# Half of each cross-attention head's probability tiles turned by VectorE in 32x32 squares and carried to their partitions by DMA

## The chip, the cores and the metric

The kernel runs on one core of one Trainium2 chip. The metric is the device time in microseconds of the whole program. The profiled execution is a separate one, with its own time.

## The reference

A decoder layer in float32 on x (8 batches, 512 tokens, 512 features) and a context of the same size: self-attention with one wide head, cross-attention with 16 heads of 64, a mixture-of-experts feed-forward, and a layer norm after each. What the change touches is the cross-attention:

```python
q = (Q @ Wq + bq).reshape(b, len_q, H, DIM_K).transpose(0, 2, 1, 3)
k = (K @ Wk + bk).reshape(b, K.shape[1], H, DIM_K).transpose(0, 2, 1, 3)
v = (V @ Wv + bv).reshape(b, V.shape[1], H, DIM_V).transpose(0, 2, 1, 3)
att = jnp.einsum('bhqd,bhkd->bhqk', q * scale, k)
att = jax.nn.softmax(att, axis=-1)
out = jnp.einsum('bhqk,bhkd->bhqd', att, v)
out = out.transpose(0, 2, 1, 3).reshape(b, len_q, H * DIM_V)
return out @ Wo + bo
```

There are 8 x 16 = 128 pairs of batch and head. Each has a 512 x 512 matrix of probabilities.

## The kernel before

Three stages run one after the other: self-attention, cross-attention (`cross_attention`), feed-forward. Float32 products are made of float32r parts: a value is split into a high part and the rest (hi and lo), and a projection takes three products of 512 columns for each of four chunks of the contraction, 12 matmuls in all.

The cross-attention goes through 16 groups (`GROUPS`; one half of the heads times one batch) of 8 heads, and a group has 16 steps, two to a head. The order is written out by hand: `SCHEDULE` gives each step at most one projection item (V, K, Q of the next heads or groups, O of the group before). In a step TensorE does the 12 matmuls of the item (`project`, L1311), the scores of two tiles of a head that is two to three steps ahead (`scores`, L1324, 4 matmuls), the products of probabilities and values of two tiles (`values`, L1348, 4 matmuls), and the turns of two tiles (`turn`, L1335, 8 transposes). A tile of scores is 128 queries x 512 keys. It goes from PSUM through VectorE (`max_tile`, L1122), ScalarE (`exp_tile`, L1019, which also sums the row), VectorE (`recip`, L1128) and GpSimd (`norm_tile`, L958) into `prob`, which holds two heads. A turned tile is 128 keys x 512 queries, made of four 128x128 transposes into one PSUM bank; ScalarE copies its high part into `pt` (`pt_hi_tile`, L1047) and VectorE the rest (`pt_lo_tile`, L1168). After a head's four `values` ScalarE (`o_first`, L1054) and VectorE (`o_second`, L1178) bring the output to `osum`, and GpSimd splits it (`split_out`, L972 and L974).

Each engine executes its own list in order and waits for semaphores. SyncE (SP) issues all DMAs: each weight pair after the projection before it (`load_pair`, L844), the copies of the keys from one half of the partitions to the other (`double_k`, L859, from SBUF to SBUF), context (L164), x1T (L841), values' weights (L172), and the loads and stores of y (L847, L851).

## Time and profile before

| | us |
|---|---|
| median of 3 runs | 1960.04 (1959.64 to 1960.54) |
| the profiled execution | 1960.26 |
| its span, first to last instruction | 1958.4 |
| TensorE busy | 1941.7 (99%) |
| VectorE busy | 1475.2 (75%) |
| ScalarE busy | 1149.4 (59%) |
| GpSimd busy | 729.5 (37%) |

Busy times of one row can overlap in a pipelined engine, so the time from one instruction's start to the next one's start says more than the mean duration. In the digit rows each digit is a fortieth of the span. Of 16 DMA engines the share is the time that packets took.

### The profile page before, as it was taken

The numbers are of one execution on the slowest core, as the hardware profiler recorded it, in microseconds if no ns is written. First come the engines' busy times: TensorE is split into PE (matmuls) and PEld (weight loads), VectorE is DVE, ScalarE is ACT, GpSimd is POOL, SyncE is SP. The second block draws the span as 40 slices with busy tenths as digits, with TensorE's granted clock in tenths as the row PEclk, the third lists the DMA queues.
The fourth block names the chain that finished last, engine by engine and source line by source line (L and its number), as shares of the span: only waits on it lengthen the run. The fifth ranks groups of instructions, "written<-read, shape, count | busy, mean of one in ns | idle before, by whom it ended". The sixth has DMA issues, their size and how long they took to land.

```text
span 1958.4 us, 29643 instructions
## 1 busy us (share of the span) xinstructions
PE 1941.7 (99%) x9856; PEld 1632.4 (83%) x9856; DVE 1475.2 (75%) x3134; ACT 1149.4 (59%) x2462; POOL 729.5 (37%) x858
## 2 busy tenths in 40 slices
PE   8999999999999999999999999999999999999998
PEld 7888888788888888888888888888888888788887
DVE  5676666787777777777777777777777788867887
ACT  5445544676666666666766666666666667632221
POOL 2322342132343433332333333333333343527763
PEclk9999999999999999999999999999999999999999
DMA  5777778863556536364553726355462636321221
GB/s 215 274 285 280 300 280 318 277 218 106 185 171 189 186 116 195 98 192 140 184 168 101 237 65 215 107 162 172 119 193 66 194 115 218 130 87 44 86 87 65
DMA packets 112086, 334.87 MB, mean 171 GB/s; under 512 B 9152, under 2 KB 9152, under 8 KB 107200
## 3 DMA queue, kind: packets, MB, share of 16 engines
q1 hardware_dynamic: 111936, 332.98, 51.2%
q8 instruction: 80, 1.31, 0.3%
q14 instruction: 70, 0.57, 0.1%
HBM read 211.31 MB, written 88.08 MB: 153 GB/s over the span
## 4 chain that ended last, share of the span: by engine, by line
PE 94%; DVE 2%; ACT 2%; issue 1%; DMA 0%; POOL 0%; ACTq 0%; DVEq 0%; POOLq 0%
PE a_proj L1311 17%; PE a_turned L1311 17%; PE a_score L1324 11%; PE a_av L1348 11%; PE a_proj L48 9%; PE a_proj L1335 5%; PE a_turned L1335 5%; PE a_proj L1739 4%; PE a_av L1739 4%; PE a_score L48 3%; PE a_av L48 3%; ACT c_prob L1019 1%; PE a_score L1714 1%; PE a_turned L1698 1%; PE a_turned L612 1%
## 5 line engine op out<-in xcount | busy, mean ns | idle before, releaser
L958 POOL TENSOR_SCALAR c_prob<-c_prob,all_rden 128x512 f32<-128x512 f32 x512 | 350.2, 698 | 881.8 <-DVE all_rden L1128 881.8
L1019 ACT ACTIVATE c_prob<-a_score,all_negmax 128x512 f32<-128x512 f32 x512 | 348.0, 685 | 211.6 <-DVE all_negmax L1122 208.8
L1122 DVE TENSOR_REDUCE all_negmax<-a_score 128x1 f32<-128x512 f32 x512 | 329.3, 685 | 186.4 <-PE a_score L1324 186.1
L1324 PE MATMUL a_score<-c_ks,c_qs 128*128 128x512 f32 x1024 | 277.6, 391 | 3.3 <-ACT c_prob L1019 3.0
L1348 PE MATMUL a_av<-c_pt,c_vs 128*128 128x512 f32 x1024 | 277.1, 391 | 0.0
L1324 PEld LDWEIGHTS a_score<-c_ks,c_qs 128*128 128x128 f32 x1024 | 190.5, 188 | 44.7 <-ACT c_prob L1019 5.9
L1348 PEld LDWEIGHTS a_av<-c_pt,c_vs 128*128 128x128 f32 x1024 | 192.0, 188 | 39.8
L1168 DVE TENSOR_TENSOR c_pt<-a_proj,c_pt 128x512 fp32r<-128x512 f32 x258 | 171.9, 686 | 27.0 <-ACT c_pt L1047 25.0
L1311 PE MATMUL a_proj<-all_second_buffer,c_wq 128*128 128x512 f32 x756 | 188.0, 397 | 0.0
L1311 PE MATMUL a_turned<-all_third_buffer,all_first_buffer 128*128 128x512 f32 x732 | 182.6, 398 | 0.0
L1168 DVE TENSOR_TENSOR c_pt<-a_turned,c_pt 128x512 fp32r<-128x512 f32 x254 | 169.1, 686 | 9.0 <-ACT c_pt L1047 5.3
L1311 PEld LDWEIGHTS a_proj<-all_second_buffer,c_wq 128*128 128x128 f32 x756 | 137.4, 188 | 26.0
L1311 PEld LDWEIGHTS a_turned<-all_third_buffer,all_first_buffer 128*128 128x128 f32 x732 | 133.0, 188 | 25.6
L1047 ACT CAST c_pt<-a_proj 128x512 fp32r<-128x512 f32 x258 | 144.8, 589 | 1.9 <-PE a_proj L1335 1.9
L1335 PE MATMUL a_proj<-all_ident,c_prob 128*128 128x128 f32 x1032 | 144.9, 272 | 0.2 <-POOL c_prob L958 0.2
L1047 ACT CAST c_pt<-a_turned 128x512 fp32r<-128x512 f32 x254 | 143.1, 593 | 1.4
L1335 PE MATMUL a_turned<-all_ident,c_prob 128*128 128x128 f32 x1016 | 142.6, 272 | 0.1
L1311 PE MATMUL a_proj<-all_first_buffer,c_wk 128*128 128x512 f32 x564 | 141.2, 399 | 0.0
L1335 PEld LDWEIGHTS a_proj<-all_ident,c_prob 128*128 128x128 f32 x1032 | 122.8, 140 | 18.1 <-POOL c_prob L958 0.5
L1335 PEld LDWEIGHTS a_turned<-all_ident,c_prob 128*128 128x128 f32 x1016 | 120.9, 140 | 18.0 <-POOL c_prob L958 0.6
L1311 PE MATMUL a_turned<-c_WO,c_op 128*128 128x512 f32 x540 | 134.9, 398 | 0.0
L1039 ACT ACTIVATE c_qs<-a_proj,all_bq 64x512 fp32r<-64x512 f32 x126 | 86.4, 686 | 71.7 <-PE a_proj L1311 70.1
(207 smaller groups left out, 3275.0 us busy)
## 6 DMA issues: line engine op xcount, KB each, us to landing
all_first_buffer<-ctxT_scratch SPq DMA_DIRECT2D x64, 512.0 KB, 7.4
c_wk<-wk_scratch SPq DMA_DIRECT2D x64, 512.0 KB, 3.8
c_wq<-wq_scratch SPq DMA_DIRECT2D x64, 512.0 KB, 6.1
all_second_buffer<-x1T_scratch SPq DMA_DIRECT2D x16, 2048.0 KB, 14.8
c_ks<-c_ks SPq DMA_DIRECT2D x128, 256.0 KB, 5.6
ctxT_scratch<-s_csp SPq DMA_DIRECT2D x8, 2048.0 KB, 7.4
c_y<-y_steps_scratch SPq DMA_DIRECT2D x16, 1024.0 KB, 6.1
y_steps_scratch<-c_y SPq DMA_DIRECT2D x15, 1024.0 KB, 10.0
```

The costliest lines, as they stand in the source:

```text
L48: ins = nc.tensor.matmul(out, stationary(s, k), moving(m, k), start=(k == 0 and s == m == HI), stop=((k, (s, m)) == last))
L958: nc.gpsimd.tensor_scalar(prob[:, n % 2, i, :], prob[:, n % 2, i, :], rden[:, n % 2, i:i + 1], 1.0, ALU.mult, ALU.mult).then_inc(p_ready, 1)
L1019: nc.scalar.activation(prob[:, n % 2, i, :], spsum[:, i % 2, :], ACT.Exp, bias=negmax[:, n % 2, i:i + 1], scale=1.0, accum_out=den[:, n % ...
L1039: nc.scalar.activation(dst, bank[rows, :], ACT.Identity, bias=bias[rows, bass.ds(G * PAIRS + j, 1)], scale=1.0).then_inc(proj_hi, 1)
L1047: nc.scalar.copy(pt[:, t % LAG, HI, :], bank_of(("T", g, t))).then_inc(pt_hi, 1)
L1122: nc.vector.tensor_reduce(negmax[:, n % 2, i:i + 1], spsum[:, i % 2, :], AX.X, ALU.max, negate=True).then_inc(smax, 1)
L1168: nc.vector.tensor_tensor(pt[:, t % LAG, LO, :], bank_of(("T", g, t)), as_f32(pt[:, t % LAG, HI, :]), ALU.subtract).then_inc(pt_lo, 1)
L1311: ins = nc.tensor.matmul(bank_of(item), l, r, start=(k == 0 and s == m == HI), stop=(k == K - 1 and (s, m) == TERMS[-1]))
L1324: ins = nc.tensor.matmul(spsum[:, i % 2, :], qs[:, j % 2, e, i * P:(i + 1) * P], ks[:, j % 2, e, m, :], start=(m == HI), stop=(m == LO))
L1335: ins = nc.tensor.transpose(bank_of(("T", g, t))[:, i * P:(i + 1) * P], prob[:, n % 2, i, k * P:(k + 1) * P], ident[:, :])
L1348: ins = nc.tensor.matmul(opsum[:, n % 2, :], vs[:, g % 2, k, n, :], pt[:, t % LAG, m, :], start=(k == 0 and m == HI), stop=(k == T - 1 and ...
L1739: ins = pe.matmul(prod[i % 2][:, which, :], x2T[u][:, s, k, i * P:(i + 1) * P], W[which][:, m, k, :], start=(k == 0 and s == m == HI), sto ...
```

## The change

The last two of a head's four tiles of keys (`FLIPPED`, 2) are no longer turned by TensorE. For 125 of the 128 heads (all but `WHOLE`, the first two and the last):

- `prob` is laid out as [P, S, T] in place of [P, T, S]: the four query tiles stand side by side, so each of them is read and written with a step of 16 bytes. This holds for the exponentials, the scaling on GpSimd, TensorE's remaining transposes, whose output in the PSUM bank has a step of 16 bytes too (`squares`), and the sum of `o_second`, which puts the order right.
- VectorE turns the keys 256 to 511 of each query tile in place in squares of 32x32 (`flip`): four transposes of 128x256 a head.
- SyncE sends the squares to their partitions (`send_flips`): sixteen DMAs a head, each 32 partitions x 2 x 128 numbers (32 KB, runs of 512 bytes) from `prob` to `landing`, half of them in each of two steps.
- ScalarE copies the landed tiles' high part (`flip_hi_tile`, two 128x512 copies from SBUF) and GpSimd subtracts (`flip_lo_tile`, two 128x512).
- `exp_tile` of a head waits until the sixteen DMAs of the head two before have landed, since they read the same half of `prob`.
- The order of TensorE changes: `turned_in` has one turned tile a step in place of two, and `valued_in` three tiles of values in the even steps and one in the odd ones, the flipped ones four steps after the head's turn has begun. `MIDDLE` is another order of the items, with Q1 in the next group.
- The loads of context, x1T, WV and WO are issued by ScalarE in pieces (`BULK`: steps 3, 4, 6 to 11) instead of by SyncE. x1T goes in four pieces.
- In the feed-forward's preparation the stores go in pieces, `pool_gate` comes later, and several semaphores `passed` are one.

```diff
-    TILES, STEPS, LEAD, LAG = T * HH, T * HH // 2, 4, 4
+    TILES, STEPS, LEAD = T * HH, T * HH // 2, 4
+    Q, TURNED, FLIPPED = 32, 2, 2
+    SQUARES = P // Q
...
-    NEXT = ["V0+", "K0+", "Q0+", "V1+", "V2+", "K1+", "Q1+"]
-    MIDDLE = ["V3", "K2", "Q2", "O0", "O1", "O2", "K3", "Q3", "O3"] + NEXT
+    NEXT = ["V0+", "K0+", "Q0+", "V1+", "K1+", "V2+"]
+    MIDDLE = ["Q1", "K2", "Q2", "V3", "O0", "O1", "K3", "Q3", "O2", "O3"] + NEXT
...
+    WHOLE = (0, 1, HH * GROUPS - 1)
+    def turned_in(g, step):
+        n, half = divmod(step, 2)
+        return [(g, T * n + k) for k in ((2 * half, 2 * half + 1) if HH * g + n in WHOLE else (half,))]
+    def valued_in(g, step):
+        n, half = divmod(step, 2)
+        tiles = [(n - 1, 1)] if half else [(n - 2, 2), (n - 2, 3), (n - 1, 0)]
+        return [x for x in (tile_of(g, *tile) for tile in tiles) if x]
...
+    def send_flips(g, n, places=range(SQUARES)):
+        head = HH * g + n
+        sp.wait_ge(flipped, T * FLIPS[head])
+        wait(sp, av_mm, T * (head - 1))
+        src = prob[:, n % 2, TURNED * P:, :].rearrange("p (k c q) i -> p c k (q i)", k=FLIPPED, c=SQUARES)
+        dst = as_f32(landing[:, head % 2, :, :]).rearrange("p k (a n) -> p a k n", a=SQUARES)
+        for a in places:
+            for c in range(SQUARES):
+                sp.dma_start(dst[c * Q:(c + 1) * Q, a], src[a * Q:(a + 1) * Q, c]).then_inc(landed[head % 2], 16)
...
+        if head:
+            send_flips(*head, range(2, SQUARES) if step % 2 else range(2))
+        if item and item[0] == "K":
+            double_k(item[1], item[2])
...
+    def flip_lo_tile(g, n, k):
+        nc.gpsimd.tensor_tensor(whole, as_f32(whole), as_f32(flip_hi_part[:, k, :]), ALU.subtract).then_inc(flip_lo, 1)
...
+    BULK = {3: [("v", (0, 1))], 4: [("v", (2, 3))], 10: [("o", (0, 1))], 11: [("o", (2, 3))], 6: [("c", 0), ("c", 1)], 7: [("c", 2), ("c", 3)], 8: [("x", 0), ("x", 1)], 9: [("x", 2), ("x", 3)]}
...
         if i == 0:
-            wait(act, t_mm, T * head - T)
-        nc.scalar.activation(prob[:, n % 2, i, :], spsum[:, i % 2, :], ACT.Exp,
+            if head - 2 in FLIPS:
+                act.wait_ge(landed[head % 2], 16 * SQUARES * SQUARES * LANDINGS[head - 2])
+        nc.scalar.activation(prob[:, n % 2, :, i], spsum[:, i % 2, :], ACT.Exp,
...
+    def flip_hi_tile(g, n, k):
+        act.wait_ge(landed[head % 2], 16 * SQUARES * SQUARES * LANDINGS[head])
+        wait(act, av_mm, T * (head - 1) + TURNED + k + 1)
+        nc.scalar.copy(flip_hi_part[:, k, :], as_f32(landing[:, head % 2, k, :])).then_inc(flip_hi, 1)
...
+    def flip(g, t):
+        dve.wait_ge(p_ready, TILES * g + t + 1)
+        block = prob[:, n % 2, TURNED * P:, i]
+        nc.vector.transpose(block, block).then_inc(flipped, 1)
...
-            ins = nc.tensor.transpose(bank_of(("T", g, t))[:, i * P:(i + 1) * P],
-                                      prob[:, n % 2, i, k * P:(k + 1) * P], ident[:, :])
+            ins = nc.tensor.transpose(squares(bank_of(("T", g, t)))[:, i], prob[:, n % 2, k * P:(k + 1) * P, i],
+                                      ident[:, :])
```

TensorE in the middle of the cross-attention, before: a step with the item Q and the beginning of the next one. Names are the written and the read tiles; `a_proj`, `a_score`, `a_turned`, `a_av` are PSUM banks.

```order
L1311 MATMUL a_proj<-all_second_buffer,c_wq 128x512 x12
L1324 MATMUL a_score<-c_ks,c_qs 128x512 x4
L1348 MATMUL a_av<-c_pt,c_vs 128x512 x4
L1335 MATMUL a_turned<-all_ident,c_prob 128x128 x8
L1311 MATMUL a_proj<-c_WO,c_op 128x512 x12
```

And after: an odd step, and then an even one.

```order
L1367 MATMUL a_proj<-c_WO,c_op 128x512 x12
L1380 MATMUL a_score<-c_ks,c_qs 128x512 x4
L1406 MATMUL a_av<-c_pt,c_vs 128x512 x2
L1390 MATMUL a_proj<-all_ident,c_prob 128x128 x4
L1367 MATMUL a_turned<-all_third_buffer,all_first_buffer 128x512 x12
L1380 MATMUL a_score<-c_ks,c_qs 128x512 x4
L1406 MATMUL a_av<-c_flip_hi,c_vs 128x512
L1406 MATMUL a_av<-c_landing,c_vs 128x512
L1406 MATMUL a_av<-c_flip_hi,c_vs 128x512
L1406 MATMUL a_av<-c_landing,c_vs 128x512
L1406 MATMUL a_av<-c_pt,c_vs 128x512 x2
L1390 MATMUL a_turned<-all_ident,c_prob 128x128 x4
```

The eight transposes of a step are now four; the 20 matmuls of 512 columns are 18 in the odd step and 22 in the even one.

SyncE (SP) before, over most of a group: the DMAs in order, with the semaphores that the first of a row waits for.

```order
L844 DMA c_wk<-wk_scratch 128x1024 [waits c_proj_mm]
L164 DMA all_first_buffer<-ctxT_scratch 128x2x512 x4
L859 DMA c_ks<-c_ks 64x1024 [waits c_proj_lo] x2
L844 DMA c_wq<-wq_scratch 128x1024 [waits c_proj_mm]
L841 DMA all_second_buffer<-x1T_scratch 128x4096
L851 DMA y_steps_scratch<-c_y 128x4x512 [waits c_wo_out]
L847 DMA c_y<-y_steps_scratch 128x4x512 [waits c_y_stored]
```

And after, in some six steps of a group, from the second half of one head's sixteen on:

```order
L903 DMA c_landing<-c_prob 32x2x128 [waits c_av_mm,c_flipped,c_proj_mm]
L903 DMA c_landing<-c_prob 32x2x128 x7
L880 DMA c_y<-y_steps_scratch 128x4x512 [waits c_y_stored]
L877 DMA c_wk<-wk_scratch 128x1024 [waits c_proj_mm]
L903 DMA c_landing<-c_prob 32x2x128 [waits c_av_mm,c_flipped]
L903 DMA c_landing<-c_prob 32x2x128 x7
L891 DMA c_ks<-c_ks 64x1024 [waits c_proj_lo] x2
L903 DMA c_landing<-c_prob 32x2x128 [waits c_av_mm,c_flipped,c_proj_mm]
```

Context and x1T are gone from this queue, and eight DMAs stand in each step, with the weights' loads ahead of them and the copies of the keys behind them.

ScalarE after, one even step and the odd step behind it:

```order
L1084 ACTIVATE c_qs<-a_turned,all_bq 64x512 [waits c_s_mm,c_proj_mm]
L1084 ACTIVATE c_qs<-a_turned,all_bq 64x512
L1064 ACTIVATE c_prob,all_den<-a_score,all_negmax 128x512 [waits c_landed1,c_t_mm,c_smax]
L1064 ACTIVATE c_prob,all_den<-a_score,all_negmax 128x512 [waits c_smax]
L1112 ACTIVATE c_opart<-a_av,all_bv 64x512 [waits c_o_sum,c_av_mm]
L1099 CAST c_pt<-a_turned 128x512 [waits c_av_mm,c_t_mm]
L1105 CAST c_flip_hi<-c_landing 128x512 [waits c_av_mm,c_landed1] x2
L1076 CAST c_vs<-a_proj 128x8x64 [waits c_proj_mm]
L1064 ACTIVATE c_prob,all_den<-a_score,all_negmax 128x512 [waits c_smax] x2
L1099 CAST c_pt<-a_proj 128x512 [waits c_av_mm,c_t_mm]
```

The exponential that waits for `landed` has everything else of ScalarE behind it.

## Rows read from the trace of the kernel before

**Rows 1.** The page: busy times, the granted clock, the DMA queue.

```profile
PE 1941.7 (99%) x9856; PEld 1632.4 (83%) x9856; DVE 1475.2 (75%) x3134; ACT 1149.4 (59%) x2462; POOL 729.5 (37%) x858
...
PEclk9999999999999999999999999999999999999999
...
q1 hardware_dynamic: 111936, 332.98, 51.2%
```

**Rows 2.** The page's chain that ended last, shares of the span by engine.

```profile
PE 94%; DVE 2%; ACT 2%; issue 1%; DMA 0%; POOL 0%; ACTq 0%; DVEq 0%; POOLq 0%
```

**Rows 3.** Line 1335 alone: duration ns min/median/max, first and last start.

```profile
L1335 PE MATMUL a_proj<-all_ident,c_prob x1032: 270/272/332, 367.5 to 1732.0; 128*128 128x128 f32 x172
...
L1335 PE MATMUL a_turned<-all_ident,c_prob x1016: 270/272/328, 366.8 to 1724.4; 128*128 128x128 f32 x170
```

**Rows 4.** Timeline, 1000 to 1015 us: start, us, engine, line, count.

```profile
1000.56 1.07 PE L1348 MATMUL a_av<-c_pt,c_vs 128*128 128x512 f32 x4
1001.25 1.02 PEld L1335 LDWEIGHTS a_turned<-all_ident,c_prob 128*128 128x128 f32 x8
...
1001.48 1.03 PE L1335 MATMUL a_turned<-all_ident,c_prob 128*128 128x128 f32 x8
...
1002.24 2.58 PEld L1311 LDWEIGHTS a_proj<-all_second_buffer,c_wq 128*128 128x128 f32 x12
1002.27 2.98 PE L1311 MATMUL a_proj<-all_second_buffer,c_wq 128*128 128x512 f32 x12
...
1005.08 1.07 PE L1324 MATMUL a_score<-c_ks,c_qs 128*128 128x512 f32 x4
```

**Rows 5.** The page's costliest groups: count, busy, mean ns.

```profile
L1019 ACT ACTIVATE c_prob<-a_score,all_negmax 128x512 f32<-128x512 f32 x512 | 348.0, 685 | 211.6 <-DVE all_negmax L1122 208.8
...
L1168 DVE TENSOR_TENSOR c_pt<-a_proj,c_pt 128x512 fp32r<-128x512 f32 x258 | 171.9, 686 | 27.0 <-ACT c_pt L1047 25.0
...
L1047 ACT CAST c_pt<-a_proj 128x512 fp32r<-128x512 f32 x258 | 144.8, 589 | 1.9 <-PE a_proj L1335 1.9
L1335 PE MATMUL a_proj<-all_ident,c_prob 128*128 128x128 f32 x1032 | 144.9, 272 | 0.2 <-POOL c_prob L958 0.2
```

**Rows 6.** Busy us of each engine in a stretch of the cross-attention.

```profile
560.00:1000.00 440.00, 440.00 (x2266) 370.43 (x2265) 336.52 (x648) 289.42 (x628) 160.83 (x219) 1.00 0.51 161
```

**Rows 7.** Groups by line and shape: the nearest to the added operations.

```profile
L974 POOL TENSOR_TENSOR c_op<-c_osum,c_op 128x512 fp32r<-128x512 f32 x60 | 77.5, 1292 | 5.0
...
L368 ACT CAST s_wsp<-s_wraw 128x512 fp32r<-128x512 f32 x32 | 17.5, 617 | 0.3
```

**Rows 8.** VectorE's groups by shape, 256 and 512 columns.

```profile
L488 DVE TENSOR_TENSOR all_x<-a_score,s_strip 128x512 f32<-128x512 f32 x8 | 5.5, 689 | 7.8 <-PE a_score L48 7.8
...
L488 DVE TENSOR_TENSOR all_x<-a_score,s_strip 128x256 f32<-128x256 f32 x8 | 3.4, 424 | 0.3
...
L517 DVE TENSOR_SCALAR s_gone<-all_x 128x256 f32<-128x256 f32 x8 | 2.2, 274 | 0.0
```

**Rows 9.** Timeline of SyncE's queue, 738 to 746 us.

```profile
738.57 0.33 SPq L844 DMA_DIRECT2D c_wk<-wk_scratch  x1
738.94 1.99 SPq L164 DMA_DIRECT2D all_first_buffer<-ctxT_scratch  x4
741.00 1.38 SPq L859 DMA_DIRECT2D c_ks<-c_ks  x2
```

**Rows 10.** The same, 966 to 973 us.

```profile
967.19 2.53 SPq L172 DMA_DIRECT2D all_third_buffer<-wv_scratch  x4
```

**Rows 11.** Line 859 alone: issue ns, and us to landing.

```profile
L859 SPq DMA_DIRECT2D c_ks<-c_ks x128: 462/468/1127, 348.6 to 1696.3; - x128
...
DMA to landing us min/median/max: 3.0/5.6/12.3
```

**Rows 12.** The page's DMA issues: count, KB each, us to landing.

```profile
y_steps_scratch<-c_y SPq DMA_DIRECT2D x4, 256.0 KB, 2.0
```

**Rows 13.** Waits from 600 to 1700 us: total, times, longest.

```profile
POOL c_prob L958 <- DVE all_rden L1128: 699.2, 205, 5.3
ACT c_prob L1019 <- DVE all_negmax L1122: 162.4, 115, 3.0
```

405 lines of the change are left out of this document (200 added, 205 removed).

## The prediction

> **What bounds the kernel now.** I read the page first. TensorE is busy for 1941.7 us of 1958.4, at full granted clock in every slice, and VectorE for 75% [rows 1]. The chain of work that ended last is TensorE for 94% [rows 2]. The busy share of a pipelined engine can flatter, so I looked at starts: in the timeline the four products with values begin at 1000.56, the eight turns at 1001.48, the next projection at 1002.27, the next scores at 1005.08, with no hole [rows 4]. In the stretch from 560 to 1000 us TensorE is busy throughout [rows 6], and in the list of waits it stands in no long row: GpSimd and ScalarE wait [rows 13]. So here time goes by TensorE's work, as long as the others stay inside it. The turns run from 366.8 to 1732.0 us in 256 steps [rows 3]; less the 0.8 us of the last step's own eight, that is 1364.4 / 255 = 5.35 us a step, 10.70 a head. A matmul of 512 columns costs (1001.48 - 1000.56) / 4 = 0.23 us between starts.
>
> **What the change removes.** 125 heads x 2 tiles x 4 = 1000 transposes. A transpose's price between weight loads is (1002.24 - 1001.25) / 8 = 0.124 us [rows 4]; between matmul starts 0.79 / 8 = 0.099; by busy time 144.9 / 1032 = 0.140 [rows 5]. I take 0.124: -124 us, ends -99 and -140. The step becomes 5.35 - 0.50 = 4.85, the head 9.70 us. Values move by two matmuls from odd steps to even ones, so even steps are about 5.3 and odd ones 4.4.
>
> **What it adds, per step, against 4.85 us.**
> VectorE: 336.52 / 440 x 5.35 = 4.09 now [rows 6]. One `pt_lo` goes, 171.9 / 258 = 0.67 [rows 5]. Two transposes of 128x256 come. No row shows one; the nearest 256-column passes take 0.274 and 0.424 us [rows 8], and twice the second, 0.85, is my upper end, 0.27 the lower. I take 0.35: 4.12. At 0.85 it would be 5.1, above TensorE.
> ScalarE: 289.42 / 440 x 5.35 = 3.52 [rows 6]; one copy from PSUM goes (144.8 / 258 = 0.56, [rows 5]), one from SBUF comes (0.62, [rows 7]), and eight DMAs a group at 0.515 (below), 0.26 a step: 3.84. Step 7 of a group is the worst: two landed tiles 1.24, a Q item some 1.4, two exponentials 2 x 348.0 / 512 = 1.36 [rows 5], a copy 0.56 and two DMA issues 1.03 make 5.6 in a step of 4.4. That lateness of 1.2 in 15 groups is 18 us if TensorE feels all of it; the steps around have room, so I take 8 (ends 0 and 18).
> GpSimd: 160.83 / 440 x 5.35 = 1.96, plus one subtraction of 1.29 [rows 7]: 3.25. It waited 699 us [rows 13]; hidden.
>
> **SyncE.** Sixteen DMAs a head are new. Four loads of context take from 738.94 to 741.00, 0.515 us each [rows 9]; four of values' weights take 2.53, 0.63 each [rows 10]; the only DMA from SBUF to SBUF there is, the copy of the keys, is 0.468 [rows 11] plus a gap of 0.04 (738.57 + 0.33 to 738.94, [rows 9]). The flips are SBUF to SBUF with a stepped second dimension. I take 0.515, by the two rows that agree; ends 0.47 and 0.65. That is 8.24 us a head. What else SyncE issues for a group is eight weight pairs at 0.37, eight copies at 0.51 and two DMAs of y like the pairs: 7.8, so 0.98 a head. Sum 9.2 of 9.70: it fits, narrowly. It stops fitting at (9.70 - 0.98) / 16 = 0.545 us an issue.
>
> **The added waits.** The sends of head n begin when the values of head n-2 are done, 20 matmuls into the head's first step, 4.6 us. Behind that wait stand the weight pairs and key copies. The sends with one weight load (0.37) and half of a pair of key copies (0.5) take 9.1: 13.7. For the landing, DMAs of 256 KB took 2.0 us at best [rows 12], the key copies 3.0 [rows 11]; for 32 KB after its issue I take 1.5 (ends 1.0 and 3.0): 15.2. The first exponential of head n+2, which must wait for that, would start by itself after two steps, 14 matmuls and a maximum: 9.7 + 3.2 + 0.7 = 13.6. So it starts 1.6 late. Behind it on ScalarE stands everything, but TensorE needs the result only at its scores a step later, at 9.7 + 5.3 + 2.8 = 17.8, so the start may be as late as 17.1. Margin 1.9 us. Also around the loop (release, the exponentials and copies of two steps, GpSimd's scaling, the flip: some 8 us with hand-offs; then 9.1 and 1.5): 18.6 for two heads, 9.3 each, under 9.70. Heads in whose steps a weight load and both key copies come, or that meet ScalarE's bulk transfers on the DMA engines, use the margin up. For these I take 0.28 us a head, 35 us (ends 0 and 110, the latter by 0.9 a head).
>
> **DMA engines.** 125 heads x 512 KB is 65.5 MB; by bytes 65.5 / 333 x 51.2% = 10% more [rows 1], hidden. By packets (125 x 16 x 64 = 128,000 of 512 bytes, beside 111,936) it would be 58% more, over the whole: that is the far end. I stay near bytes.
> The Trainium skill ("DMA: Bandwidth & Descriptors", Why small descriptors are slow) says that SBUF-to-SBUF transfers do not suffer the penalty of small descriptors; no row here shows runs of 512 bytes between partitions.
>
> **Sum.** The profiled execution, 1960.3 (0.2 over the median): - 124 + 8 + 35 = 1879 us.
>
> **Stepped access.** The exponential's output, the scaling, the flips, the weight loads of the remaining transposes and their output in PSUM now step by 16 bytes. No row shows such an access. I price it at nothing, as all rows are of contiguous ones; the other end is that each such element takes twice the time.
> The Trainium skill ("SBUF — State Buffer", Door 1: The DMA port swizzle) says that accesses want at least two hits in a 16-byte line of SBUF and that any non-contiguous pattern in PSUM slows matmuls significantly. With fp32 and a step of 16 bytes every access would be to another line. No row here can weigh it; it speaks against the change, for the rival next.
>
> **Rivals.**
> 1. Stepped access costs. If the eight transposes that a head keeps take 0.248 instead of 0.124, TensorE's head is again 9.70 + 0.99 = 10.69, what it was. An element costs VectorE (689 - 424) / 256 = 1.04 ns [rows 8]; with as much on ScalarE an exponential takes 0.5 us more: 3.84 + 1.0 = 4.9 a step; VectorE some 0.27 more a flip and 0.27 a step for the sum: 4.9. Nobody has slack, and the loop grows by four exponentials' 2.0 and 0.6 elsewhere, to 10.6 a head. Time 1960 to 1990; I say 1975. If only half of it holds, about 1925. For it: nothing measured. Against it: nothing measured.
> 2. SyncE becomes the bound. At the row with 0.645 us from start to start (2.53 us and its gap, for four, [rows 10]) a head costs 16 x 0.645 + 0.98 = 11.3 us against 10.70 before: 125 x 0.6 = 75 us slower, 2035. It decides against the change from (10.70 - 0.98) / 16 = 0.607 us an issue. For it: that row has the same stepped form, and landing times of up to 12.3 us show queues [rows 11]. Against it: the other two rows.
> 3. VectorE becomes the bound: transposes of 0.85 make its step 5.12, 0.27 over TensorE's: 250 x 0.27 = 68 us above the forecast, 1947. For it: VectorE has the largest share beside TensorE. Against it: a pass of 256 columns takes half of that.
>
> **Chances.** Forecast 0.41 (own range 1845 to 1925); stepped access 0.26, of which 0.06 still faster, 0.04 within, 0.16 slower; SyncE or the DMA engines 0.21, slower; VectorE 0.12, of which 0.05 faster, 0.01 within, 0.06 slower (the sum of stepped access on top). A measurement of this kernel tells 0.2%, 4 us, from no change. Faster 0.52, within 0.05, slower 0.43. The range takes in the -140 with nothing lost below and the SyncE case above: 1840 to 2040.
>
> **What would show it.** Right: TensorE's step at 4.85, four transposes in 0.5 us between the weight loads' starts; L903 at 0.5 us from start to start; the exponential's wait for `landed` short, with TensorE not waiting for it; VectorE's transposes at 0.3 to 0.4. Wrong: weight loads of L1390 well above 140 ns or exponentials above 685 ns (rival 1); SyncE issuing without a pause and TensorE idle behind ScalarE's exponential (rival 2); VectorE busy for over 95% of a step (rival 3). If TensorE idles for long, the granted clock in its row may leave 9; a chain with much less TensorE than 94% would say so as well.

## The result and the profile after

The changed kernel takes 2300.16 us (2297.74 to 2303.30, four runs) against 1960.12 for the kernel before in the same comparison: a ratio of 1.1735, 95% interval 1.1721 to 1.1749. The forecast was 1879 us with a range up to 2040. It failed by 421 us and in its sign.

| us | before | after |
|---|---|---|
| span of the profiled execution | 1958.4 | 2300.2 |
| TensorE busy | 1941.7 (99%) | 2022.9 (88%) |
| VectorE busy | 1475.2 (75%) | 1651.6 (72%) |
| ScalarE busy | 1149.4 (59%) | 1329.6 (58%) |
| GpSimd busy | 729.5 (37%) | 1298.9 (56%) |

The page of the changed kernel, the rows that answer to [rows 1]:

```profile
PE 2022.9 (88%) x8856; PEld 1579.2 (69%) x8856; DVE 1651.6 (72%) x3384; ACT 1329.6 (58%) x2462; POOL 1298.9 (56%) x1108
...
PEclk9999999899999999999999999999999899889999
...
DMA packets 288932, 400.58 MB, mean 174 GB/s; under 512 B 42112, under 2 KB 170112, under 8 KB 286592
...
q1 hardware_dynamic: 252864, 329.44, 45.3%
```

TensorE is busy for longer although a tenth of its instructions is gone, and no engine is busy for over 88%: everything waits for something. The chain that ended last, which was TensorE for 94% [rows 2]:

```profile
PE 34%; SPq 34%; DVE 10%; DMA 8%; issue 6%; ACT 6%; POOL 2%; ACTq 1%; POOLq 0%; DVEq 0%
SPq L903 30%; DMA c_landing<-c_prob 8%; PE a_proj L48 8%; PE a_turned L1367 4%; ACT c_prob L1064 4%; PE a_proj L1789 4%; PE a_av L1789 4%; DVE all_negmax L1183 3%; PE a_score L48 3%; PE a_av L48 2%; DVE c_prob L1237 2%; PE a_score L1380 2%; SPq L877 2%; DVE c_osum L1246 2%; PE a_proj L1367 2%
```

A third of it is now SPq, the issue of transfers on SyncE's queue, and nearly all of that is line 903, the sends. The costliest groups, which answer to [rows 5, 7]:

```profile
L985 POOL TENSOR_SCALAR c_prob<-c_prob,all_rden 128x512 f32<-128x512 f32 x512 | 608.6, 1214 | 644.6 <-DVE all_rden L1189 644.3
L1064 ACT ACTIVATE c_prob<-a_score,all_negmax 128x512 f32<-128x512 f32 x512 | 564.5, 1176 | 580.0 <-DMA c_landing<-c_prob 500.7
L1380 PE MATMUL a_score<-c_ks,c_qs 128*128 128x512 f32 x1024 | 351.9, 446 | 210.4 <-ACT c_prob L1064 208.4
...
L992 POOL TENSOR_TENSOR c_landing<-c_landing,c_flip_hi 128x512 fp32r<-128x512 f32 x250 | 318.7, 1298 | 12.7 <-ACT c_flip_hi L1105 11.9
...
L1237 DVE STREAM_TRANSPOSE c_prob<-c_prob 128x256 f32<-128x256 f32 x500 | 303.1, 651 | 26.4 <-POOL c_prob L985 26.1
L1246 DVE TENSOR_TENSOR c_osum<-a_av,c_opart 64x512 f32<-64x512 f32 x128 | 141.9, 1109 | 61.6 <-ACT c_opart L1112 61.4
...
L1105 ACT CAST c_flip_hi<-c_landing 128x512 fp32r<-128x512 f32 x250 | 143.1, 625 | 0.0
...
L1390 PEld LDWEIGHTS a_turned<-all_ident,c_prob 128*128 128x128 f32 x532 | 93.8, 202 | 67.1 <-POOL c_prob L985 54.4
```

Two things stand here. ScalarE's exponential waited 500.7 us for landings, and the scores 208.4 us for the exponential. And every operation that steps by 16 bytes is longer: the exponential 1176 ns against 685, the scaling 1214, the sum of `o_second` 1109, the flip 651, the weight loads of the turns 202. The operations that do not step are as priced: the copy of a landed tile 625, GpSimd's subtraction 1298.

The busy times of the stretch from 700 to 1700 us, in the columns of [rows 6]:

```profile
700.00:1700.00 1000.00, 865.18 (x3646) 651.11 (x3644) 734.50 (x1367) 646.49 (x1175) 628.75 (x539) 0.96 0.58 168
```

Less TensorE (865 of 1000 against 440 of 440), and a granted clock of 0.96 where it was 1.00, in a stretch in which the engine pauses for the exponential. A matmul of the scores takes 446 ns here in the mean, 391 before. What part of the lost time is the lower clock, and not the pauses before it, no run separates. Line 903 alone (issue ns min/median/max, who waited, landing):

```profile
L903 SPq DMA_DIRECT2D c_landing<-c_prob x2000: 585/597/2087, 395.0 to 2059.3; - x182
...
  ACT c_prob L1064: 500.7, 107
...
DMA to landing us min/median/max: 1.8/2.3/9.6
```

The issues themselves stand in the timeline of SyncE and ScalarE around 1200 us (start, us, engine, line, count), as [rows 9, 10] for before:

```profile
1198.98 8.96 SPq L903 DMA_DIRECT2D c_landing<-c_prob  x14
...
1207.99 0.59 SPq L880 DMA_DIRECT2D c_y<-y_steps_scratch  x1
...
1208.62 0.50 SPq L877 DMA_DIRECT2D c_wk<-wk_scratch  x1
1209.22 5.08 SPq L903 DMA_DIRECT2D c_landing<-c_prob  x8
1209.30 1.17 ACT L1064 ACTIVATE c_prob<-a_score,all_negmax 128x512 f32<-128x512 f32 x1 [3.37 <-DMA c_landing<-c_prob]
...
1210.87 2.39 POOL L985 TENSOR_SCALAR c_prob<-c_prob,all_rden 128x512 f32<-128x512 f32 x2 [3.37 <-DVE all_rden L1189]
```

Fourteen sends take 8.96 us, eight take 5.08: 0.64 us from start to start, and the neighbours, a load of y and of a weight pair, are as close. From 700 to 1700 us the trace holds 1402 transfers of SyncE, 1221 of them sends, and the pauses between them sum up to 66 us. So 16 x 1000 / 1221 = 13.1 us a head against 10.70 before, and (13.1 - 10.7) x 125 = 300 of the 340 us that were lost. The exponential at 1209.30 has waited 3.37 us for the landing of the head two before, whose last send was issued at 1207.35 and landed 1.8 us later: it waits for SyncE to get through its list. VectorE's reciprocal and GpSimd's scaling wait behind it. The list of waits from 700 to 1500 us, which answers to [rows 13] (total, times, longest), has that at the top:

```profile
ACT c_prob L1064 <- DMA c_landing<-c_prob: 241.5, 55, 12.4
DVE all_rden L1189 <- ACT c_prob L1064: 149.9, 69, 9.5
PEld a_score L1380 <- ACT c_prob L1064: 131.2, 117, 8.7
```

### The profile page after: what moved, and what is told of

Its sections match the earlier page's. It is cut to its first block, busy times and chain, and to the rows that moved or that the text cites. A ratio compares the mean times of both kernels' runs of the same rounds, so it can differ in the third digit from the quotient of the medians.

```text
span 2300.2 us, 30421 instructions
## 1 busy us (share of the span) xinstructions
PE 2022.9 (88%) x8856; PEld 1579.2 (69%) x8856; DVE 1651.6 (72%) x3384; ACT 1329.6 (58%) x2462; POOL 1298.9 (56%) x1108
## 2 busy tenths in 40 slices
DMA packets 288932, 400.58 MB, mean 174 GB/s; under 512 B 42112, under 2 KB 170112, under 8 KB 286592
## 4 chain that ended last, share of the span: by engine, by line
PE 34%; SPq 34%; DVE 10%; DMA 8%; issue 6%; ACT 6%; POOL 2%; ACTq 1%; POOLq 0%; DVEq 0%
SPq L903 30%; DMA c_landing<-c_prob 8%; PE a_proj L48 8%; PE a_turned L1367 4%; ACT c_prob L1064 4%; PE a_proj L1789 4%; PE a_av L1789 4%; DVE all_negmax L1183 3%; PE a_score L48 3%; PE a_av L48 2%; DVE c_prob L1237 2%; PE a_score L1380 2%; SPq L877 2%; DVE c_osum L1246 2%; PE a_proj L1367 2%
## 5 line engine op out<-in xcount | busy, mean ns | idle before, releaser
L985 POOL TENSOR_SCALAR c_prob<-c_prob,all_rden 128x512 f32<-128x512 f32 x512 | 608.6, 1214 | 644.6 <-DVE all_rden L1189 644.3
L1064 ACT ACTIVATE c_prob<-a_score,all_negmax 128x512 f32<-128x512 f32 x512 | 564.5, 1176 | 580.0 <-DMA c_landing<-c_prob 500.7
L1380 PE MATMUL a_score<-c_ks,c_qs 128*128 128x512 f32 x1024 | 351.9, 446 | 210.4 <-ACT c_prob L1064 208.4
L992 POOL TENSOR_TENSOR c_landing<-c_landing,c_flip_hi 128x512 fp32r<-128x512 f32 x250 | 318.7, 1298 | 12.7 <-ACT c_flip_hi L1105 11.9
L1237 DVE STREAM_TRANSPOSE c_prob<-c_prob 128x256 f32<-128x256 f32 x500 | 303.1, 651 | 26.4 <-POOL c_prob L985 26.1
L1246 DVE TENSOR_TENSOR c_osum<-a_av,c_opart 64x512 f32<-64x512 f32 x128 | 141.9, 1109 | 61.6 <-ACT c_opart L1112 61.4
L1367 PE MATMUL a_turned<-all_second_buffer,c_wq 128*128 128x512 f32 x564 | 146.5, 410 | 0.0
L1105 ACT CAST c_flip_hi<-c_landing 128x512 fp32r<-128x512 f32 x250 | 143.1, 625 | 0.0
L1367 PE MATMUL a_proj<-all_third_buffer,all_first_buffer 128*128 128x512 f32 x564 | 141.1, 399 | 0.6 <-DVE c_ks L1208 0.6
L1367 PEld LDWEIGHTS a_turned<-all_second_buffer,c_wq 128*128 128x128 f32 x564 | 107.5, 198 | 21.1
L1064 ACT ACTIVATION_READ_ACCUMULATOR c_prob<-a_score,all_negmax 128x1 f32 x512 | 111.1, 217 | 0.0
```

The source lines that it names most:

```text
L985: nc.gpsimd.tensor_scalar(prob[:, n % 2, :, i], prob[:, n % 2, :, i], rden[:, n % 2, i:i + 1], 1.0, ALU.mult, ALU.mult).then_inc(p_ready, 1)
L992: nc.gpsimd.tensor_tensor(whole, as_f32(whole), as_f32(flip_hi_part[:, k, :]), ALU.subtract).then_inc(flip_lo, 1)
L1064: nc.scalar.activation(prob[:, n % 2, :, i], spsum[:, i % 2, :], ACT.Exp, bias=negmax[:, n % 2, i:i + 1], scale=1.0, accum_out=den[:, n % ...
L1237: nc.vector.transpose(block, block).then_inc(flipped, 1)
L1246: nc.vector.tensor_tensor(osum[rows, n // 2, :].rearrange("p (i a q) -> p i a q", i=T, a=SQUARES), squares(opsum[DK:P, n % 2, :]), squares ...
L1367: ins = nc.tensor.matmul(bank_of(item), l, r, start=(k == 0 and s == m == HI), stop=(k == K - 1 and (s, m) == TERMS[-1]))
```

## The experiments

Every kernel ran beside the kernel before on the same chip (1960.0 to 1960.8 us). The theories at the start: SyncE's queue is full; the sends land late or are slow for another reason; the 16-byte step. "Does not cross" below means that the squares stay in their partitions. The stretches and lists of waits are from 700 to 1500 us.

### 1. Fewer transfers, the step alone, the order alone

`one_send`: the sixteen sends of a head become one of the same bytes, which does not cross, issued in the head's second step. `four_sends`: four of them, one for each 32 partitions.

```diff
-        for a in places:
-            for c in range(SQUARES):
-                sp.dma_start(dst[c * Q:(c + 1) * Q, a], src[a * Q:(a + 1) * Q, c]).then_inc(landed[head % 2], 16)
+        if 0 in places:
+            return
+        sp.dma_start(as_f32(landing[:, head % 2, :, :]),
+                     prob[:, n % 2, TURNED * P:, :].rearrange("p (k m) i -> p k (m i)", k=FLIPPED)).then_inc(
+                         landed[head % 2], 16)
```

> Left out: the squares are not carried across partitions; one DMA a head of 128 partitions carries the same 512 KB in place of the sixteen. All else is the changed kernel. SyncE theory (SyncE's list of DMAs, at 0.64 to 0.68 us each, sets the pace of 13.1 us a head): SyncE's work falls from some 12.4 to under 3 us a head, TensorE's own work becomes the bound at some 10.0 us a head, time 1850 to 1930, ScalarE waits for landed under 30 us in all. Stepped-access theory (the slower exponentials, scalings and sums set the pace): time stays over 2150. Latency theory (the round from a head's landing to the next but one's flips is too long, whatever SyncE does): between the two, 2000 to 2150, and ScalarE still waits for landed.

> Left out: crossing partitions; four DMAs a head of 32 partitions x 2 x 512 numbers, each to its own partitions, two in each step, the same bytes. SyncE theory: 4 x 0.65 + 1.6 = 4.2 us a head on SyncE, no bound, within 1% of the kernel with one send. Latency theory: a quarter of the way from it to 2300, some 2000. Stepped access: over 2150. It also shows what a 32-partition DMA of four times the bytes takes to issue: 0.6 if it goes by the DMA, 1.2 or more if it goes by bytes or runs.

Measured: 2022.4 us, ratio 1.0323 (1.0307 to 1.0340), and 2061.5, ratio 1.0518 (1.0502 to 1.0533). One transfer in place of sixteen is worth 278 us, but neither comes below the kernel before, where the SyncE theory had put one_send. Both lie near the latency theory's times (2000 to 2150, and some 2000). In one_send SyncE pauses for some 850 of 1000 us, and ScalarE still waits for landings:

```profile
ACT c_prob L1064 <- DMA c_landing<-c_prob: 70.1, 17, 6.6
```

`before_stepped` is the kernel before with only the layout of the change (in SBUF, in the bank in PSUM, and in the sum).

```diff
-    prob = sc.sb("prob", [P, 2, T, S])
+    prob = sc.sb("prob", [P, 2, S, T])
-        nc.scalar.activation(prob[:, n % 2, i, :], spsum[:, i % 2, :],
+        nc.scalar.activation(prob[:, n % 2, :, i], spsum[:, i % 2, :],
...
```

> The kernel before with only the changed kernel's layout: probabilities with the query tile innermost (steps of 16 bytes), transposes into PSUM with the same step, the sum that puts the order right. Nothing left out, no flips. SyncE theory: exponentials 1.0 us apart in place of 0.68, but TensorE stays the bound and grows by what the stepped transposes take, 8 x 0 to 0.04 us a step: 1960 to 2045. Stepped-access theory: most of the 340 us is here, 2200 or more.

Measured: 2004.8 us, ratio 1.0229 (1.0214 to 1.0244), within the SyncE theory's range. The step alone costs 44 us where TensorE is the bound. Its page has TensorE's busy time and these groups:

```profile
PE 1971.8 (98%) x9856; PEld 1669.7 (83%) x9856; DVE 1537.6 (77%) x3134; ACT 1339.2 (67%) x2462; POOL 981.7 (49%) x858
```

```profile
L1019 ACT ACTIVATE c_prob<-a_score,all_negmax 128x512 f32<-128x512 f32 x512 | 571.8, 1189 | 210.4 <-DVE all_negmax L1122 208.9
...
L1337 PEld LDWEIGHTS a_proj<-all_ident,c_prob 128*128 128x128 f32 x1032 | 151.6, 208 | 13.8 <-POOL c_prob L958 4.1
```

The turns from 700 to 1500 us (TensorE's busy time and count, its weight loads' busy time and count, clock, DMA share and GB/s), first before, then here:

```profile
700.00:1500.00 800.00, 152.28 (x1176) 137.10 (x1176) 1.00 0.49 152
```

```profile
700.00:1500.00 800.00, 160.90 (x1152) 161.52 (x1152) 1.00 0.48 150
```

At eight a step that is 147 steps and 144, 5.44 us a step and 5.56, and TensorE is busy for 800.00 of 800 us in both. So some 20 to 30 of the 44 us are TensorE's own turns, eight of which take 0.87 us in place of 0.79 to the start of the next projection. The rest falls in the first and the last groups, which have fewer items for TensorE; from 1690 us to the end of the turns it is busy for 76 of 86 us.

`all_whole` was meant as the order alone: the change with `WHOLE = tuple(range(HH * GROUPS))`, no flips and no sends.

> The changed kernel with every head whole: no flip and no send, all transposes on TensorE, but its order of TensorE, its layout and ScalarE's issuing of the bulk loads. Nothing left out. SyncE theory: like the kernel before with the stepped layout, within 1.5%. A theory that the new order or ScalarE's bulk loads cost: over 2100.

Measured: 2201.3 us, ratio 1.1235 (1.1216 to 1.1254). The number is the second theory's (over 2100), but the list of waits shows another stall, which whole heads alone have in this order, since two of their tiles use buffers that the order releases late:

```profile
ACT c_flip_hi L1099 <- PE a_av L1406: 111.9, 64, 8.0
```

So it says nothing on the flipped heads, and it is no control. `straight_early` below, which has the new order and ScalarE's loads too, is faster than the kernel before, so these two are not what costs.

### 2. The step in the changed kernel, twelve sends, and the way through DRAM

`straight_one` is one_send with the layout of the kernel before. `twelve_sends` keeps the bytes and does not cross.

```diff
         for a in places:
-            for c in range(SQUARES):
-                sp.dma_start(dst[c * Q:(c + 1) * Q, a], src[a * Q:(a + 1) * Q, c]).then_inc(landed[head % 2], 16)
+            for c in range(2):
+                sp.dma_start(dst[a * Q:(a + 1) * Q, c], src[a * Q:(a + 1) * Q, c]).then_inc(landed[head % 2], 16)
+            sp.dma_start(...).then_inc(landed[head % 2], 16)
```

> The changed kernel with one transfer a head (2x512 numbers of all 128 partitions, which stay in their partitions, so the squares do not cross) and with the probabilities held as before, 512 neighbouring numbers for each query tile, instead of every fourth number. It differs from the run with one transfer a head by the 16-byte step alone. Theory A, what one transfer left above the kernel before (62 us) is the step in the accesses of ScalarE, GpSimd, VectorE and of TensorE's weight loads (44 us in the kernel before): the four transposes taken from each head then pay at last, and the time is 1880 to 1960 us, exponential and scaling back at 0.69 and 0.70 us, a flip near 0.35. Theory B, it is the new order and the wait for the landing: 2000 us or more, whatever the step.

> The changed kernel with twelve transfers a head instead of sixteen, the same bytes, each from 32 partitions to the same 32 partitions (the squares do not cross), eight of one square pair and four of two. Theory A, SyncE's queue is a threshold: 12 x 0.64 = 7.7 us and some 1.5 to 2 us for its other transfers are 9.2 to 9.7 us a head, under the 10.7 to 11 us a head that the kernel with four transfers takes (2061 us), so twelve cost nearly nothing: 2050 to 2110 us, SyncE with gaps again. Theory B, each transfer delays the landing that ScalarE waits for, and the time grows in proportion from four (2061) to sixteen (2300): 2220 us.

Measured: 1975.2 us, ratio 1.0074 (1.0054 to 1.0093), and 2140.5, ratio 1.0922 (1.0906 to 1.0938). The step costs 47 us here; 96 us are still missing to the forecast. Twelve sends lie between both theories (under 2110, 2220): SyncE pauses again, some 200 of 1000 us, and yet a head takes 12 x 1000 / 1013 = 11.85 us. So a full queue is not the whole price. The timeline of straight_one shows what else there is:

```profile
1000.32 7.33 SPq L901 DMA_DIRECT2D c_landing<-c_prob  x2
...
1011.75 0.69 ACT L1063 ACTIVATE c_prob<-a_score,all_negmax 128x512 f32<-128x512 f32 x1 [8.51 <-DMA c_landing<-c_prob]
```

One send a head, and the exponential waits 8.51 us. The two sends of the first row are of two heads, issued at 1000.32 and 1007.02. The exponential waits for the first; its issue and landing alone:

```profile
L901 SPq DMA_DIRECT2D c_landing<-c_prob x1: 818/818/818, 1000.3 to 1000.3; - x1
...
DMA to landing us min/median/max: 11.3/11.3/11.3
```

SyncE issues it in the head's second step, behind its wait for that step's projection, and then it takes 11.3 us to land, where the median is 5.0. A weight pair, issued just before, and four loads of context that ScalarE issued from 997.1 to 1002.2 (512 KB each, up to 9.3 us to landing) were in flight beside it. That they made it late is likely and not shown by itself. In the change the last eight sends stand behind that same wait for a projection.

`dram_stepped` and `dram_blocked` do the whole computation with five transfers a head: a write to DRAM, four reads. The second holds the probabilities in blocks of 128 neighbouring numbers.

```diff
+            sp.dma_start(passing[head % 2], prob[:, n % 2, TURNED * P:, :]...).then_inc(written[head % 2], 16)
+        src = passing[head % 2].rearrange("(a q) (k c n) -> c q k a n", a=SQUARES, k=FLIPPED, c=SQUARES)
+        for c in range(SQUARES):
+            sp.dma_start(dst[c * Q:(c + 1) * Q], src[c]).then_inc(landed[head % 2], 16)
```

> The whole computation, with the squares sent by way of DRAM: one transfer writes the head's flipped 128 x 1024 numbers to a scratch of DRAM in the first step, four read them back in the next (32 partitions each, pieces of 512 bytes), so five transfers a head instead of sixteen, every fourth number as in the change. Theory A (number of transfers on SyncE's queue): 5 x 0.6 = 3 us a head, and it comes out within 2% of one transfer a head, 1985 to 2065 us. Theory B (the crossing of partitions in 512-byte pieces is what is slow, or the way through DRAM lands too late): above 2120 us, with ScalarE waiting for the landing.

> The whole computation by way of DRAM with five transfers a head, and the probabilities held in blocks of 128 neighbouring numbers, so no engine steps by 16 bytes, but the pieces that are read back are 128 bytes long instead of 512 (4096 a head). Theory A (transfers on the queue, and the step): both are gone, 1880 to 1960 us, the first to beat the kernel before. Theory B (short pieces occupy the DMA engines): the landing comes late, over 2050 us, with the DMA engines' share well above that of the 512-byte pieces.

Measured: 2096.9 us, ratio 1.0696 (1.0680 to 1.0712), and 2147.6, ratio 1.0950 (1.0932 to 1.0969). Both are better than the change by 150 us and more, and both lose to the kernel before: dram_stepped falls between its theories, dram_blocked is theory B's (the DMA engines' share is 0.85, against 0.75).

### 3. Issued a step earlier

`straight_early` is straight_one with the send in the head's first step; `early_light` is the same with only an eighth of the bytes of the context's and x1T's loads.

```diff
-        if 0 in places:
+        if 0 not in places:
             return
```

> The run with one transfer a head and neighbouring numbers (1975 us; the squares do not cross), with that transfer issued one step earlier, in the head's first step as soon as its four flips are done, instead of in the second. Theory A, what is left above the kernel before is the landing that comes late for ScalarE (it waited for it 101 us of 800, 17 times up to 10.1 us): a step more of room (4.9 us) takes most of it, 1890 to 1935 us. Theory B, another wait (VectorE, or the order of the steps) bounds it: 1960 us or more.

> The run with the early transfer, with ScalarE's loads of the context and of x1T cut to the first 64 of each 512 columns (the rest of the operand is left from before), so that an eighth of these bytes is in flight. Theory A, the landing comes late where it shares the DMA engines with these 4 MB a group: the waits for the landing go altogether, 1870 to 1910 us, and at least 20 us less than the run with the whole loads. Theory B, these loads do not matter to the landing: within 0.5% of that run.

Measured: straight_early 1885.5 us, ratio 0.9617 (0.9603 to 0.9631); early_light 1878.4, ratio 0.9582 (0.9567 to 0.9596). One step is worth 90 us (straight_early ends 5 us under theory A's range), the landing waits are gone (3.2 us in all), a landing takes 3.9 us at the median in place of 5.0, and what the loads add beyond that is 7 us: theory B of early_light, A had said at least 20. The stretch from 700 to 1500 us of straight_early, its turns (first and last start), and its chain:

```profile
700.00:1500.00 800.00, 799.68 (x3824) 660.17 (x3824) 668.85 (x1434) 575.88 (x1233) 491.23 (x557) 1.00 0.66 217
```

```profile
L1389 PE MATMUL a_turned<-all_ident,c_prob x532: 270/272/421, 367.5 to 1649.2; 128*128 128x128 f32 x178
```

```profile
PE 92%; DVE 4%; DMA 1%; ACT 1%; POOL 1%; issue 1%; ACTq 0%; POOLq 0%; DVEq 0%
```

TensorE is the bound again, at (1649.2 - 367.5 - 0.5) / 255 = 5.02 us a step. This is the kernel that the prediction had described, but its squares do not cross and nothing steps by 16 bytes. The turns alone from 700 to 1500 us, and the timeline around one step's four:

```profile
700.00:1500.00 800.00, 95.61 (x640) 79.30 (x640) 1.00 0.66 217
```

```profile
1002.23 0.60 PE L1389 MATMUL a_turned<-all_ident,c_prob 128*128 128x128 f32 x4
1002.58 3.02 PE L1366 MATMUL a_proj<-all_third_buffer,all_first_buffer 128*128 128x512 f32 x12
```

At four a step that is 160 steps, 5.00 us each against 5.44 before: 0.44 us less. The four turns take 0.35 us to the next projection, where the eight took 0.79 [rows 4]: 0.44 again.

`stepped_early` is the same with the 16-byte step.

> The change with one send a head (its squares do not cross) issued in the head's first step, every fourth number as in the change. It is the run straight_early (1885 us) with the 16-byte step. Theory A, the step costs what it cost with the late send (2022 - 1975 = 47 us) and in the kernel before (44 us): 1925 to 1945 us. Theory B, the late send hid part of it, or the longer accesses use up the slack of VectorE and ScalarE and the two costs add up to more: above 1955 us.

Measured: 1967.7 us, ratio 1.0041 (1.0026 to 1.0056), theory B. Its stretch, chain and turns:

```profile
700.00:1500.00 800.00, 779.43 (x3654) 648.06 (x3653) 735.64 (x1373) 659.67 (x1183) 621.84 (x536) 1.00 0.62 204
```

```profile
PE 55%; DVE 17%; POOL 17%; issue 6%; ACT 3%; DMA 1%; ACTq 0%; POOLq 0%; SPq 0%; DVEq 0%
```

```profile
L1390 PE MATMUL a_turned<-all_ident,c_prob x532: 270/283/421, 367.7 to 1731.0; 128*128 128x128 f32 x178
...
  POOL c_prob L985: 82.5, 126
```

VectorE is busy for 92%, no landing is waited for, and the turns wait for GpSimd's scaling: 5.35 us a step in the mean of the whole stage, what it was before. The step alone eats the whole gain.

### 4. Sends that nobody waits for, before and behind the one that counts

`idle_fifteen` is straight_early with fifteen further transfers a head behind it (32 partitions of the identity to DRAM); in `late_fifteen` the one that counts stands behind them.

```diff
+        for a in range(7) if 0 in places else range(7, 15):
+            sp.dma_start(idle[head % 2, a], ident[Q * (a % SQUARES):Q * (a % SQUARES) + Q, :]).then_inc(
+                idle_sent[head % 2], 16)
```

> The same as the run with the early transfer, and behind it on SyncE's queue fifteen more a head that nobody waits for: 32 partitions of the identity (512 bytes each) to a scratch of DRAM, seven in the head's first step and eight in its second. Their bytes are a quarter of a square pair's. Theory A, the issue of sixteen transfers fills SyncE's queue, whoever waits for them: (16 + about 3 others) x 0.62 to 0.66 is 11.8 to 12.5 us a head, and the weights, the doubled keys and the next head's transfer come late: 2120 to 2260 us. Theory B, it is the landing of the sends themselves (32 partitions crossing, their latency) that costs: within 2% of the run without them.

> The run with fifteen idle sends a head (1974 us; neighbouring numbers, squares do not cross), with the one send that counts moved from before the fifteen to behind them. The queue holds the same sixteen. Theory A, a full queue and a landing late in it are two separate costs: ScalarE's exponential now waits for a landing that is issued some 8 us later, and the time is 2040 to 2200 us. Theory B, only the fullness of the queue counts: within 1% of 1974 us.

Measured: 1973.8 us, ratio 1.0064 (1.0047 to 1.0081): 88 us, between both theories. And 2073.6 us, ratio 1.0577 (1.0562 to 1.0593), theory A. Both lists of waits, first of idle_fifteen, then of late_fifteen:

```profile
ACT c_prob L1068 <- DMA c_landing<-c_prob: 92.3, 26, 6.0
...
PE a_turned L1371 <- DMA c_wq<-wq_scratch: 14.1, 7, 2.9
```

```profile
ACT c_prob L1069 <- DMA c_landing<-c_prob: 225.9, 59, 10.3
```

These transfers are cheaper to issue (median 0.422 us) than the sends (0.597), and so the queue is only just full: 31 us of pauses in 1000, at 15 x 1000 / 1391 = 10.8 us a head. The next head's send and a weight pair come late. The DMA engines' share is 0.74 as well, against 0.66 without the fifteen; this run does not separate the two. In late_fifteen the send costs 100 us more, with ScalarE's wait at 226 us of 800. But there it is also issued in the head's second step, and that alone had cost 90 us with an empty queue (straight_one). So the 100 us are mostly the step's, and lateness (90) and a full queue (88) add up to what late_fifteen lost, 188 us.

### 5. The sixteen real sends, put otherwise

`all_at_once`: all sixteen in the head's first step. `blocked`: blocks of 128 neighbouring numbers, no step, pieces of 128 bytes.

```diff
-            send_flips(*head, range(2, SQUARES) if step % 2 else range(2))
+            if step % 2 == 0:
+                send_flips(*head)
```

> The change, with all sixteen sends of a head in its first step, ahead of that step's doubled keys, instead of eight in the first and eight in the second. Theory A, SyncE's queue holds 16 x 0.68 + 2.4 x 0.64 = 12.4 us of issue a head whatever the order: within 1.5% of the change, 2265 to 2335 us. Theory B, it is the landing that is late and not the queue: the last send is issued earlier and it takes under 2250 us.

> The whole computation with all sixteen sends, and the probabilities in blocks of 128 neighbouring numbers, so that no engine steps by 16 bytes; the sends then move pieces of 128 bytes instead of 512. Theory A, SyncE's queue sets the pace and the step of 16 bytes is hidden behind it: within 2% of the change, 2255 to 2340 us, though exponential, scaling and o_second are back at 0.7 us and the flip is at 0.42. Theory B, the step is on the path there too: 47 us or more less, under 2255 us. Theory C, four times the pieces make the sends land later: above 2340 us.

Measured: 2241.0 us, ratio 1.1426 (1.1405 to 1.1447), theory B narrowly; and 2306.3, ratio 1.1767 (1.1749 to 1.1784), theory A. To have no send behind the second step's projection is worth 59 us; part of it can be the granted clock, 0.98 there from 700 to 1700 us against 0.96 in the change. In blocked the flips and exponentials are short again and the time stays; its sends start every 0.73 us instead of 0.68, and the clock from 700 to 1700 us is 0.92, both of which may cover a gain, so that the step costs nothing there is likely and not shown.

`split_stepped` and `split_blocked`: eight sends by SyncE in the first step, eight in pairs by ScalarE between its instructions.

> The whole computation, with the sixteen sends of a head divided between two queues: eight by SyncE in the head's first step, eight by ScalarE in pairs between its instructions of the two steps, every fourth number as in the change. Theory A, SyncE's queue and the landing behind it: SyncE then has 8 x 0.68 + 2.4 x 0.6 = 6.9 us a head, the landing comes some 5 us earlier, ScalarE's issues overlap its own work, and what is left is TensorE with the 16-byte step: 1920 to 1990 us. Theory B, ScalarE pays for its issues in full (7.3 us of work a head and 8 x 0.6 = 4.8 us make 12.1 us a head): 2180 us or more. Theory C, crossing partitions with sixteen small transfers is slow on the DMA engines themselves: above 2100 us with SyncE idle and ScalarE waiting for the landing.

> The same division of the sends over the two queues, with the probabilities in blocks of 128 neighbouring numbers (sends in pieces of 128 bytes). Theory A: no step, so 30 to 50 us less than the stepped one, 1885 to 1950 us, under the kernel before. Theory B, ScalarE pays in full: 5.8 + 4.8 = 10.6 us a head, 2010 us or more. Theory C, the four times smaller pieces bring the landing late: slower than the stepped one.

Measured: 2236.4 us, ratio 1.1407 (1.1390 to 1.1424), and 2133.9, ratio 1.0876 (1.0858 to 1.0894). Theory B's times for both. Line 902 and the chain of split_stepped:

```profile
L902 ACTq DMA_DIRECT2D c_landing<-c_prob x1000: 592/617/2034, 394.9 to 1991.5; - x167
L902 SPq DMA_DIRECT2D c_landing<-c_prob x1000: 585/619/2198, 394.9 to 1991.1; - x167
...
DMA to landing us min/median/max: 1.8/2.0/7.4
```

```profile
PE 30%; ACT 22%; ACTq 21%; DVE 12%; issue 10%; DMA 3%; SPq 1%; POOL 1%; POOLq 0%; DVEq 0%
ACTq L902 20%; ACT c_prob L1064 15%; PE a_proj L48 8%; DVE all_negmax L1196 5%; DVE c_pt L1242 4%; PE a_proj L1802 4%; PE a_av L1802 4%; DMA c_landing<-c_prob 3%; ACT c_pt L1099 3%; PE a_score L48 3%; PE a_av L48 2%; PE a_proj L1380 2%; DVE c_prob L1250 2%; PE a_av L1419 1%; ACT c_flip_hi L1105 1%
```

ScalarE and its queue are 43% of the chain, and the exponential hardly waits for a landing any more (11 us of 800): the queue has moved, not gone. But ScalarE does not pay in full. From 700 to 1500 us it issues for 373 us; it is busy for 551 us, and for 731 with the issuing taken in, so about half of the issuing runs beside the instruction before. Crossing partitions is not what is slow: the landing's median is 2.0 us here and 2.3 in the change, and 2.3 to 2.5 in twelve_sends, which does not cross.

`dram_early`: the way through DRAM, write and reads both in the first step.

> The whole computation by way of DRAM (2097 us when the four reads were issued in the head's second step), with write and reads both in the first step, the reads behind that step's doubled keys. Theory A, the landing was late there by the step: the price falls as it did for one send (90 us), towards the early single send with the 16-byte step plus what the longer way adds: 1935 to 2010 us; a time under 1960 would be the first whole computation that beats the kernel before. Theory B, SyncE stands waiting for the write (some 2.5 us a head) and the DMA engines carry 1 MB more a head, so the reads land late all the same: 2040 us or more.

Measured: 2110.3 us, ratio 1.0752 (1.0731 to 1.0773), theory B. Issuing earlier did not help here. The waits from 700 to 1500 us, and the reads' issue and landing:

```profile
ACT c_flip_hi L1114 <- DMA c_landing<-passing_scratch: 108.6, 43, 7.7
```

```profile
L909 SPq DMA_DIRECT2D c_landing<-passing_scratch x500: 557/608/1562, 397.6 to 1876.3; - x167
...
DMA to landing us min/median/max: 2.6/3.0/12.2
```

Median 3.0 us, but up to 12.2. No version that computes the whole beat the kernel before.

## Why the prediction was wrong

| from one to the next | us | change |
|---|---|---|
| before | 1960 | |
| one early transfer, neighbouring numbers | 1885 | -75 |
| the same with the 16-byte step | 1968 | +82 |
| sixteen sends that cross in its place (all_at_once) | 2241 | +273 |
| half of them a step later: the change | 2300 | +59 |

**The step that failed: SyncE's issue price.** I took 0.515 us from a load from DRAM and a copy of the keys and wrote that it "fits, narrowly", up to 0.545, and that the sign turns at 0.607. Measured is 0.64 at the median from start to start, 0.68 in the mean. The other transfers, priced at 0.37 and 0.51, cost as much once they stand back to back. From 700 to 1700 us a head has 1402 / 76.3 = 18.4 transfers at (1000 - 66) / 1402 = 0.67 us, 12.3 us, and its share of the pauses makes 13.1. The row that was right was the one I put at the end of the range, the four loads with a stepped second dimension at 0.645 [rows 10], and "by the two rows that agree" was no reason: neither had the form of the new transfer. Rival 2 had the mechanism, but at 11.3 us a head and 75 us: the neighbours at their new price are 0.6 us more, the sends at 0.67 instead of 0.645 another 0.4, and the pauses, which it left out, 0.9.

**The added wait.** I had a margin of 1.9 us and 35 us of cost. With 16 x 0.64 the last send is issued 2.0 us later than in my chain and it lands after 2.3 us at the median, not 1.5: the margin is gone before any collision. The runs give the size: the same one send costs 90 us more when issued a step later, and 88 more when fifteen others fill the queue behind it. And twelve sends cost 173 us more than one early send (2141 against 1968) although they leave SyncE 20% idle.

**Stepped access, priced at nothing.** That all rows were contiguous was no reason for that price. It costs 44 us in the kernel before, 47 with one late send, 82 with one early send: the tighter the rest, the more. What it costs in the change itself is not shown. Rival 1's sizes were near (an exponential +0.49 us against my 0.5, a flip +0.22 against 0.27, VectorE at 735.64 / 800 x 5.35 = 4.92 us a step against 4.9), and its time too, 1975 against 1968. But TensorE's turns were the smaller part: a matmul went from 272 to 283 ns, a weight load from 140 to some 200, and a turn from start to start from 0.099 to 0.109 us, not to 0.248. By the chain of stepped_early the rest was VectorE and GpSimd, 17% each.
The Trainium skill ("SBUF — State Buffer", Door 1: The DMA port swizzle) was right that such accesses cost, and the rows give 1.5 to 1.7 times for ScalarE, GpSimd and VectorE. That a non-contiguous pattern in PSUM slows matmuls significantly the turns bear out weakly: a tenth from start to start, with the weight loads' slower reads of SBUF in it.

**The other terms.** The removed transposes: 5.35 to 5.02 us a step in the mean is 0.33 x 250 = 83 us of the 124 taken, under my lower end of 99. In the middle, where TensorE is full, the step shrank by 0.42 to 0.44, which is 106 to 110 us over 250 steps: 0.11 for a transpose, between my starts of matmuls (0.099) and of weight loads (0.124). The rest went at the ends. From first turn to first turn a middle group of 16 items takes 87.1 us before and 80.3 here, but the first and the last group, which have 21 items together in both kernels, take 146 us before and 154 here. TensorE has less to do there and pauses (it is busy for 64 of the last 72 us). The 5.35 was a mean over both kinds of group; a step of the middle took 5.44. The flip without the step is 0.434 at the median against 0.35 (ends 0.27 and 0.85). GpSimd was hidden while nothing stepped. The DMA engines were no bound: 288932 packets and a share of 0.58; in blocked, with pieces of 128 bytes, the landing's median was 2.4 us against 2.3. The lower end of my range, 1840, does not follow from its reason: with -140 and nothing lost the time is 1820.
The Trainium skill ("DMA: Bandwidth & Descriptors", Why small descriptors are slow) exempts SBUF-to-SBUF transfers from the small descriptors' penalty; by the landings the trace agrees, though in blocked the DMA engines' share from 700 to 1700 us is 0.67 against 0.58.

That straight_early came to 1885 against the 1879 of the forecast is luck: two errors cancel, 41 us less gained and 43 us of waits that did not come, and behind the last turn it takes 6 us more than the kernel before (232 against 226). It also leaves out what the forecast had to price, the crossing.

## What to carry to other kernels

Price the issue of many small transfers by a row of the same form that stands back to back with others, and multiply every transfer on that queue by it. Where a buffer is freed by the last of several transfers, that queue's time is a latency too, and it costs long before the queue is full. A layout that makes one transfer possible is paid by every engine that touches the data, so try it alone in the kernel before.
